# Two-layer graph network on one core: where the attention reads its banks, in the first two groups of each head

## The reference

```
Wh = (H @ W).reshape(n, N_HEADS, D_K)
e = leaky_relu(sl[:, :, None] + sr.T[None, :, :], 0.2)   # sl, sr: Wh . a_l, Wh . a_r
e = where(mask, e, -inf);  alpha = softmax(e, axis=2)
out = elu(einsum('nhm,mhd->nhd', alpha, Wh))
```

## Time and profile before

| | us |
|---|---|
| median of 3 runs | 886.37 |
| lowest, highest | 883.03, 889.32 |
| the profiled execution | 884.81 |
| its span, from first to last instruction | 883.2 |
| busy: PE, DVE, ACT, POOL | 824.4, 727.9, 688.8, 154.4 |

### The profile page before, as it was taken

One profiled execution on the slowest core, in us unless ns is written; L12 is line 12 of the kernel. 1 busy time (PEld: TensorE's weight loads), 2 busy tenths in 40 slices (PEclk: granted clock), 3 DMA queues, 4 the chain that ended last, 5 costly groups with the idle time before them and its releaser, 6 DMA issues.

```text
span 883.2 us, 26730 instructions
## 1 busy us (share of the span) xinstructions
PE 824.4 (93%) x10276; PEld 658.7 (75%) x10276; DVE 727.9 (82%) x1403; ACT 688.8 (78%) x966; POOL 154.4 (17%) x221
## 2 busy tenths in 40 slices
PE   3998899999999999869899999999999999999996
PEld 3444455555555555449899999999999999899996
DVE  3897587777778777587888999888999889998885
ACT  3676557676666666488999989899989999898993
POOL 0111355454546463300000000000000000000000
PEclk9999899999999999979999999999999999999999
DMA  7346768778787878640041011221101410111011
GB/s 220 119 142 218 276 244 299 294 288 306 286 303 280 308 278 304 102 105 26 0 95 48 0 48 48 46 49 48 48 0 47 95 48 0 47 47 48 0 24 36
DMA packets 74907, 115.33 MB, mean 131 GB/s; under 512 B 55584, under 2 KB 57504, under 8 KB 66688
## 3 DMA queue, kind: packets, MB, share of 16 engines
q1 hardware_dynamic: 67504, 94.19, 32.3%
q0 software_dynamic: 7376, 20.85, 7.7%
HBM read 98.17 MB, written 16.85 MB: 130 GB/s over the span
## 4 chain that ended last, share of the span: by engine, by line
PE 57%; DVE 19%; ACT 9%; issue 7%; DMA 5%; DVEq 1%; SPq 1%; ACTq 0%
PE ps_a L576 11%; PE ps_x L639 10%; PE ps_t L639 10%; PE ps_a L639 10%; PE ps_w L639 5%; PE ps_h L639 5%; DMA stage<-in_adj 5%; ACT stage L787 5%; DVE stage L1069 3%; DVE bits L961 3%; PE ps_x L534 1%; DVE stage L1059 1%; DVE mT L1080 1%; PE ps_t L562 1%; PE ps_a L534 1%
## 5 line engine op out<-in xcount | busy, mean ns | idle before, releaser
L576 PE MATMUL ps_a<-g,mT 128*128 128x512 f16 x1024 | 235.2, 384 | 2.5 <-DVE mT L972 2.5
L787 ACT ACTIVATE stage<-bits,sr 128x1024 int8<-128x1024 f32 x192 | 205.8, 1160 | 11.3 <-PE ps_w L639 10.9
L787 ACT ACTIVATE stage<-rows,sr 128x1024 int8<-128x1024 f32 x192 | 204.5, 1165 | 5.2 <-PE ps_w L639 5.1
L576 PEld LDWEIGHTS ps_a<-g,mT 128*128 128x128 fp8e4 x1024 | 101.1, 99 | 112.9 <-issue 7.8
L727 ACT ACTIVATE junk<-bits 128x2048 uint8<-128x2048 uint8 x64 | 122.3, 1910 | 68.1 <-DVE bits L961 63.3
L1069 DVE SCALAR_TENSOR_TENSOR stage<-stage,mask 128x1024 int32<-128x1024 int32 x128 | 156.1, 1219 | 19.2 <-ACT stage L787 19.0
L1080 DVE TENSOR_SCALAR mT<-stage 128x1024 int32<-128x1024 int32 x128 | 88.0, 687 | 29.1 <-PE ps_w L639 28.6
L639 PE MATMUL ps_x<-g,stage 128*128 128x130 f16 x1024 | 79.6, 220 | 14.8 <-DVE late L1121 10.6
L961 DVE TENSOR_SCALAR bits<-stage 128x2048 uint8<-128x2048 int32 x64 | 78.8, 1262 | 11.2 <-DMA stage<-in_adj 11.0
L639 PE MATMUL ps_t<-g,stage 128*128 128x130 f16 x1024 | 80.9, 220 | 0.1
L639 PE MATMUL ps_a<-g,stage 128*128 128x130 f16 x1024 | 80.6, 221 | 0.0
(11 more groups left out here) (144 smaller groups left out, 1284.5 us busy)
## 6 DMA issues: line engine op xcount, KB each, us to landing
stage<-in_adj SPq DMA_DIRECT2D x64, 1024.0 KB, 6.7
mask<-in_x SPq DMA_DIRECT2D x16, 256.0 KB, 2.7
own_scratch<-mask POOLq DMA_DIRECT2D x16, 256.0 KB, 3.0
rows<-in_x POOLq DMA_DIRECT2D x32, 128.0 KB, 3.1
rows<-own_scratch POOLq DMA_DIRECT2D x32, 128.0 KB, 5.4
x_scratch<-late POOLq DMA_DIRECT2D x32, 128.0 KB, 2.1
bits<-s_scratch SPq DMA_DIRECT2D x8, 512.0 KB, 4.6
rows<-s_scratch SPq DMA_DIRECT2D x8, 512.0 KB, 5.1
```

The source lines that it names most:

```text
L576: last = nc.tensor.matmul(ps_a[e][:, :], m[:, kk, b, :], g[:, 2 * kk + b, :], start=(kk == 0 and b == 0), stop=(kk == NK - 1 and b == 1))
L787: nc.scalar.activation(sign_bytes(sgn, k, b), srow[gr % 2], ACT.Sign, bias=sr[:, 2 * k + b, H + gr // NS:H + gr // NS + 1]).then_inc(act_s ...
```

## The change

It has two parts, and neither adds nor removes an instruction that computes.

DVE: where `gr % 4` is 0 or 1 (groups 1, 4, 5, 8, 9, 12 and 13), the eight reads of the group before come at the end of step 0, right behind the pos of step 0. Before, they came in step 1, behind the AND of step 1 and the sign of step 2. In groups 2, 3, 6, 7, 10, 11, 14 and 15 nothing changes.

ACT: in group 1 alone, the reads come behind the first sign of step 1. Before, they came behind all three signs of step 1 and the first of step 2.

```diff
@@ ACT @@
             for gr in range(1, NG):
                 for q in range(NQ):
-                    if q != 2:
-                        signs(gr, q)
-                    if q == 1:
+                    if q == 1 and gr == 1:
+                        signs(gr, 1, 1)
+                        read_minus(gr - 1)
+                        signs(gr, 1, 1, True)
+                    elif q == 1:
+                        signs(gr, 1)
                         signs(gr, 2, 1)
                         read_minus(gr - 1)
-                    if q == 2:
+                    elif q == 2 and gr > 1:
                         signs(gr, 2, 1, True)
+                    else:
+                        signs(gr, q)
                     if q == (7 if gr % NS == 0 else 5):
                         exps(gr - 1)
@@ DVE @@
                     z_of(gr, q)
                     signs(gr, q + 1)
-                    if q == 1:
-                        if gr == 1:
-                            dve.wait_ge(fac_halved, 1)
+                    if q == 1 and not reads_early(gr):
                         read_plus(gr - 1)
...
                     pos_of(gr, q)
+                    if q == 0 and reads_early(gr):
+                        if gr == 1:
+                            dve.wait_ge(fac_halved, 1)
+                        read_plus(gr - 1)
...
+def reads_early(gr):
+    return gr % NS in (0, 1)
```

## The result

The changed kernel takes **880.48 us** (median of 7, 875.54 to 882.38), the kernel before 886.37 (median of 7, 883.03 to 890.96). The ratio is 0.991, with a 95% interval from 0.988 to 0.994. By the medians the kernel is 5.9 us faster, clear of noise, and short of the 1% that I had put at 877.5. The interval of the ratio stands for 5.5 to 10.5 us. In a later comparison, with 8 and 20 executions, it is 881.39 against 888.53, ratio 0.991 (0.988 to 0.994). The forecast was 877.0, the range 873.5 to 882.5.

The account below looks back on a forecast made before the run. TensorE, 93% busy, was taken as held up at group starts by VectorE's late bank reads. Gains of 2.8 + 1.75 + 2.31 + 1.75 = 8.6 gave 876.2 or 877.8, forecast 877.0 us, range 873.5 to 882.5.

Parts of the forecast that it names:

- PE's restart of group 1: Start of group 1: PE restarts at 422.07, not 424.58, after a stop of about 0.5 us instead of 2.90.
- The stop at group 2: Start of group 2: ACT's extra signs delay the reads, a new stop of about 0.9 us; gain there still 2.8.
- the new stop at step 5: Pos of step 5 in groups 4, 8 and 12: PE stops about 1.51 us, DVE's values coming no earlier.
- the sign of being wrong: Step 1 of all seven early-read groups: forecast wrong if PE stops for the AND, held to be covered.
- PE comes 1.79 earlier, DVE doesn't: Group 4, model for 8 and 12: reads start 1.79 us earlier, DVE's instructions from pos of step 1 keep their times.
- Rival (c): Groups 4 to 13 gain nothing because DVE is the bound; group 1 alone pays, 882.0 us; chance 0.08.
- The sum: Whole attention: 2.8 at groups 1 and 2, then 1.75, 2.31 and 1.75 at the three heads, 8.6 us.
- the whole 0.27: Starts of groups 5, 9 and 13: 0.27 us gained because DVE's reads no longer set PE's pace.
- rival (a): Clock falls at the new step-5 stops; two falls give 880.1 us, three 881.7; chance 0.25.
- (b): More comes back: other executions' clock falls vanish, or step 5 isn't late, 0.3 us a head; 873 us; chance 0.12.
- (d): Slower: at all seven starts each read waits for ACT's, 0.50 us a bank instead of 0.26; 889.5; chance 0.05.
- (e): Nothing measurable is left because falls of the clock elsewhere cover it, 884 to 887 us; chance 0.03.

Follow-up runs that it names:

- first-only kernel: Against the changed kernel, DVE's early reads only in groups 1, 4, 8 and 12, not 5, 9 and 13; attention length 491.19 us, ratio 0.996.
- pos-first kernel: Against the changed kernel, the pos of step 5 goes ahead of the high and low halves in groups 4, 8, 12; median 878.37 us, ratio 0.990.
- The last kernel: Changed kernel plus early reads in group 2, pos of step 5 ahead of halves, denominators, division and last result operations later; median 876.65 us, ratio 0.986.

## Why the prediction was right

**Direction, mechanism and size of the gain.** Right, step by step. PE's restart of group 1, seen from the start of the attention, was forecast at 422.07 - 388.45 = 33.62 and came at 425.99 - 392.37 = 33.62. That of group 2 was forecast at 63.9 and came at 63.80. The stop at group 2 (0.9 forecast) was 0.59 in the profile's count and 0.75 from start to start. Group 4 restarted 0.50 behind DVE's first read (514.56 to 515.05), and the new stop at step 5, forecast at 1.51, is 1.31 in the profile's count. Counted from start to start it is 1.47: PE's last visit before it began at 535.07, the next could have begun 0.23 later, and 536.77 is 1.47 behind that. PE didn't stop for the AND of step 1 in any group, which was to be the sign of being wrong. In group 1, where I had given that AND 0.2 us to spare, it ended 0.34 before PE used it, which with 0.16 for the hand-over leaves 0.18:

```profile
428.42 1.22 DVE L1074 SCALAR_TENSOR_TENSOR stage<-stage,mask 128x1024 int32<-128x1024 int32 x1 [0.75 <-ACT stage L787]
```
```profile
429.98 0.62 PE L639 MATMUL ps_x<-g,stage 128*128 128x130 f16 x8
```

**Step 5 as the limit.** "PE comes 1.79 earlier, DVE doesn't" is what the first-only kernel showed by itself (nothing gained at a head), and the pos-first kernel showed that it isn't one late instruction. The last kernel bears it out: with part of DVE's work moved out of groups 4, 8 and 12, the stops are gone. Rival (c) had the right cause, DVE as the bound from group 3 to group 5, and the wrong consequence: DVE's last late work before group 5 is the read, and that one did move.

**The sum.** 8.6 forecast, 8.22 measured, 0.4 too much. The two heads without a fall gave 1.71 and 1.50 for 1.75 each. The visits behind the restart of group 5 still follow DVE's reads in part: the eight matmuls from 546.31 took 0.54 to the next start instead of 0.45, where I had given back the whole 0.27. That explains about 0.1 a head; what else makes the 0.4 is open.

**Clock.** I had taken no fall at the new stops. No profile shows one behind the stops of 1.2 to 1.3 us at step 5; rival (a) didn't come. Over all profiles, stops of PE in the attention behind group 0:

| length of the stop | stops | followed by a fall |
|---|---|---|
| 1.01 to 1.39 | 28 | 0 |
| 1.84 to 2.02 | 9 | 3 |
| 2.41 to 5.12 | 3 | 3 |

In the stop of 5.12 us the clock fell while PE still stood, in the others behind it. So the choice of zero held for the stops that came, 1.23 to 1.34 us at step 5; between 1.39 and 1.84 there is none in the table. The Trainium skill's warning ("TensorE: Matmul & The Clock Gate", A second HAM failure mode) did not come true at this length: PE stops briefly at three heads and its clock stays at 2.4 GHz.

**What was off: the base.** The forecast of 877.0 was 3.5 too low, and the weak step is "the profiled execution took 884.81, so 876.2 against its own time", set "between" that and 877.8. The profiled execution had the second earliest start of the attention of all twelve, 388.45 where the mean is 392.2. By an estimate from these profiles, with the mean start the kernel before would take 392.2 + 494.75 + 1.6 = 888.5, and the later comparisons have 888.5 to 889.2 as its median; the changed one 392.2 + 486.5 + 1.6 = 880.3, and it has 880.5 and 881.4. I had one profile and three times, and took the profile's start for a fixed part. The first comparison's own median of before, 886.37, lies 2 us below this estimate; that it has only seven executions is the likely reason, and not shown to be. Most of its lead of 3.9 us over the changed kernel's profile was won at the last load of the adjacency matrix, with the stop and the fall of the clock behind it, as shown above. From the median alone the forecast would have been 877.8; the measured 880.48 lies within the 1%, to which I had given 0.50.

**Rivals (b), (d), (e).** (d) is out: in the changed kernel DVE's reads follow each other by 0.26 (pairs at 545.07, 545.59 and 546.12 in group 5), though ACT began only at 544.5 there, two banks ahead. (e) is out by the intervals. Of (b), the stop at step 5 came, so its second half is out. Its first half did not show either: three falls in nine stops of 1.84 to 2.02 us are one to the three such stops of the kernel before, the one that its profile had and the sum already counts.

## What to carry to other kernels

An instruction that opens a buffer for another engine belongs ahead of any work of its engine that is needed later, but only where that engine is behind; where it is ahead, moving it makes it wait, and the wait comes back as lateness. Before counting on such a move, follow the other work of the late engine at its absolute times up to the next rendezvous: what the fast engine gains is cut off at the first instruction whose margin is smaller than the gain. And measure a change in one stage by that stage's own length in several profiles: here the part ahead of it varied by 8.5 us over twelve profiles, as much as the change was worth.

## What the runs showed of the hardware

GpSimd can slow VectorE: with a pair of GpSimd products of 3.97 us under way, a VectorE sign with one tensor input takes 1.55 us instead of 0.75, so that with 24 instructions taken off VectorE it is busier (729.7 us against 727.5). It goes both ways: the pair at 578.81, beside which VectorE stood idle for 1.17 us, took 2.07. The Trainium skill says that the two engines share a pair of ports, which one of them holds for a whole instruction ("SBUF — State Buffer", Who interferes with whom). The trace agrees in the main: the lengthened sign and `add_x1` end at 506.49 and 507.95, each 0.55 us behind the end of the GpSimd product that it overlaps (505.94 and 507.40), as if they had stood for it. But the AND at 503.80, with two tensor inputs, kept its 1.22 us beside the same product, while the one at 580.11 took 1.85: not every instruction beside a product is lengthened, and what decides it was not tested.

A stop of PE between 1.84 and 2.02 us was followed by a fall of the clock in three of nine cases, in stops that look alike: of six stops of 1.91 to 1.94 us one was followed by a fall, as were those of 1.84 and 2.02, and that of 1.87 was not.
